# A macaron layer with routed experts: first FFN in groups of 1, 2, 3 and 2 sequences, a new order of loads and weight splits, ranks from products

## The chip, the core and the metric

The kernel runs on one core of a Trainium2 chip. The metric is the time of one execution on the device, in microseconds (us). A core has TensorE (PE, matrix products), VectorE (DVE), ScalarE (ACT), GpSimd (POOL) and SyncE (SP), each with its own instruction stream; they meet only at semaphores. DMA engines move data between the main memory and the on-chip memory.

## What is computed

```python
x = x + 0.5 * ffn(layernorm(x), gate_w, w1, w3, w2)
x = x + attn(layernorm(x), time_mix_k, time_mix_v, time_mix_r, time_decay, time_first, Wk, Wv, Wr, Wo)
x = x + 0.5 * ffn(layernorm(x), gate_w, w1, w3, w2)

def ffn(x, gate_w, w1, w3, w2):              # 8 experts, the best 2 of each token
    probs = softmax(x @ gate_w)
    expert_weights, expert_indices = top_k(probs, 2)
    expert_weights = expert_weights / expert_weights.sum(-1)
    for i in range(8):
        wi = where(expert_indices == i, expert_weights, 0).sum(-1)
        out += ((silu(x @ w1[i]) * (x @ w3[i])) @ w2[i]) * wi

def attn(x, ...):                            # linear attention with decay
    k, v, r = projections of x mixed with x shifted by one token
    # scan over the tokens: aa, bb, pp carry the weighted sums and their exponent
    return (sigmoid(r) * wkv(k, v)) @ Wo
```

x is 8 sequences of 512 tokens with 128 channels, the inner width of an expert 512, all float32. The layer norm has neither scale nor shift.

## The kernel before

Each token takes part in two experts, so its normalised row is copied twice into a list in main memory (`rows_in`) that is sorted by expert. The list is cut into tiles of 128 rows of one expert. A tile is loaded, turned (`turn_tile`, tensor pT), multiplied with w1 and w3 (`up`, tensors pa and pb), gated (`h`, L844) and multiplied with w2 (`down`, py); its rows go to `rows_out`, are gathered by token (L542) and added to x with their weights (`combine`, L854). The weights w1 and w3 are split into a high and a low float16 part first, ScalarE making the high one (`split_weights`, L570) and VectorE the low one (L827).

Sequences are handled in runs, each with its own list: `FIRST = (2, 2, 2, 2)` sequences in the first FFN, `SECOND = (3, 3, 2)` in the second. A run of 2 has 23 tiles, one of 3 has 31, one of 1 has 15: 177 tiles in seven runs. Before a run's first tile all of its rows must be in its list, and the list is filled with zeros first, since experts leave gaps. Runs share the four lists: run 4 uses that of run 0, run 5 that of run 1.

The routing of a run is the chain `pick`, `pick2` (best two experts on VectorE), `count` (TensorE: a product with a triangle of ones gives each token's rank within its block, one with all ones the totals), `place`, `place2` (VectorE: a running sum over blocks and experts, then each token's slot, L789), `scatter` (GpSimd, L528: for each block of 128 tokens and each of two choices one indirect DMA, 8 per sequence), `tiles` and `weights`. It needs `stats`, `rsqrt`, `norm`, `turn`, `logits`, `keep` of all its sequences. Between the two FFNs each sequence goes through the attention, the chain `MIX` from `combine` to `add` (L887 to L925 on VectorE), and the routing of runs 4 to 6 takes sequences only after it.

The order is made by `make_plan()` ahead of time, with costs in `COST` and allowances in `ROOM`: it walks over the tiles and puts steps behind them. What I call the list of a tile is the steps put behind it. Engines follow this order strictly: TensorE, ScalarE, VectorE and SyncE run `in_order`: tile, list, tile. The planner moves no tile on to within two of a run's start while that run's scatters are not given out, so a late routing makes one long list. GpSimd runs `TRANSFERS` in order; each has a gate, the number of products `h` that must be done. The steps marked `EARLY` come before the first tile. SyncE (L433) issues x, small inputs, zeros, staged weights, w2, the other zeros and x, then loads and stores of tiles; the load of a run's first tile waits for all of its scatters and is issued three loads ahead, so the stores behind it wait too. `rsqrt` (L693) is a chain of 13 small VectorE instructions, each waiting for the one before (`link`).

## Time and profile before

| | us |
|---|---|
| median of 3 runs | 689.54 (688.97 to 691.28) |
| the profiled execution | 690.3, its span 688.5 |
| TensorE busy | 518.2 (75% of the span) |
| VectorE busy | 430.6 (63%) |
| ScalarE busy | 334.9 (49%) |
| GpSimd busy | 264.7 (38%) |
| first product of a tile (`h`) starts | 75.74 |
| last one starts | 654.05 |

Times in the profile count from the span's start. A busy TensorE is a TensorE with matmuls under way. "Idle before" in brackets says how long an engine had been idle before an instruction, and what released it. An indirect DMA by GpSimd takes that engine about a microsecond of its own and lands later.

### The profile page before, as it was taken

The numbers are of one execution on the slowest core, as the hardware profiler recorded it, in microseconds if no ns is written. First come the engines' busy times: TensorE is split into PE (matmuls) and PEld (weight loads), VectorE is DVE, ScalarE is ACT, GpSimd is POOL, SyncE is SP. The second block draws the span as 40 slices with busy tenths as digits, with TensorE's granted clock in tenths as the row PEclk, the third lists the DMA queues.
The fourth block names the chain that finished last, engine by engine and source line by source line (L and its number), as shares of the span: only waits on it lengthen the run. The fifth ranks groups of instructions, "written<-read, shape, count | busy, mean of one in ns | idle before, by whom it ended". The sixth has DMA issues, their size and how long they took to land.

```text
span 688.5 us, 16328 instructions
## 1 busy us (share of the span) xinstructions
PE 518.2 (75%) x5128; PEld 462.3 (67%) x5128; DVE 430.6 (63%) x1314; ACT 334.9 (49%) x717; POOL 264.7 (38%) x267
## 2 busy tenths in 40 slices
PE   0300789899989889987962359989879989999920
PEld 0200679889878689765961139977769989999920
DVE  4490488675647599426987959786678683425402
ACT  0640546545584744777442435654856544444400
POOL 1067007556634320134101742415451547246244
PEclk9999999999999999999995579999998999999975
DMA  8991113223322222112100122221222333334222
GB/s 278 345 304 50 49 41 98 86 85 95 89 69 73 55 58 63 50 45 50 53 12 7 51 76 62 79 59 48 69 61 68 86 97 113 89 97 109 79 57 65
DMA packets 87564, 58.88 MB, mean 86 GB/s; under 512 B 9792, under 2 KB 81216, under 8 KB 87488
## 3 DMA queue, kind: packets, MB, share of 16 engines
q1 hardware_dynamic: 79296, 41.05, 20.3%
q0 software_dynamic: 8192, 16.79, 8.6%
q8 instruction: 50, 0.82, 0.5%
q14 instruction: 26, 0.21, 0.1%
HBM read 28.65 MB, written 29.16 MB: 84 GB/s over the span
## 4 chain that ended last, share of the span: by engine, by line
PE 26%; DVE 11%; POOL 6%; issue 5%; ACT 4%; DMA 2%; POOLq 0%; DVEq 0%; ACTq 0%
PE py L966 9%; PE pa L953 7%; PE pb L953 7%; POOL rows_in L528 4%; DVE h L844 2%; POOL yg L542 2%; DVE xres L854 1%; PE pT L941 1%; ACT L590 1%; ACT xn L608 1%; DMA rows_in<-parts,slot 1%; ACT sil L590 1%; DVE shared L915 1%; DMA rin<-rows_in 1%; DVE stats L687 0%
## 5 line engine op out<-in xcount | busy, mean ns | idle before, releaser
L844 DVE TENSOR_TENSOR h<-sil,pb 128x512 f32<-128x512 f32 x177 | 120.8, 687 | 177.7 <-ACT sil L590 130.7
L528 POOL DMA_INDIRECT rows_in<-parts,slot x128 | 136.9, 1070 | 210.4 <-DVE slot L789 81.7
L542 POOL DMA_INDIRECT yg<-rows_out,slot x128 | 125.9, 984 | 205.7 <-DVE h L844 158.4
L966 PE MATMUL py<-ffn_w,h 128*128 x1416 | 195.3, 282 | 7.6 <-ACT yrow L584 7.5
L966 PEld LDWEIGHTS py<-ffn_w,h 128*128 128x128 f32 x1416 | 175.1, 195 | 12.2 <-issue 8.2
L953 PE MATMUL pa<-rT,ffn_w 128*128 128x128 f16 (+1 forms) x1440 | 151.6, 248 | 21.1 <-ACT rT L579 10.9
L953 PE MATMUL pb<-rT,ffn_w 128*128 128x128 f16 (+1 forms) x1440 | 153.7, 247 | 0.0
L953 PEld LDWEIGHTS pa<-rT,ffn_w 128*128 x1440 | 114.5, 100 | 38.5 <-issue 26.9
L953 PEld LDWEIGHTS pb<-rT,ffn_w 128*128 x1440 | 114.7, 99 | 9.6
L590 ACT ACTIVATE sil<-pa 128x512 f32<-128x512 f32 x177 | 104.9, 593 | 22.5 <-PE pa L953 21.9
L584 ACT ACTIVATE yrow<-py 128x128 f32<-128x128 f32 x177 | 49.0, 277 | 114.3 <-PE py L966 113.1
L579 ACT ACTIVATE rT<-pT 128x512 f16<-128x512 f16 (+1 forms) x120 | 57.9, 482 | 85.1 <-PE pT L941 85.0
L941 PE MATMUL pT<-ident,rin 128*128 128x128 f16 x354 | 40.1, 222 | 49.9 <-DMA rin<-rows_in 49.9
L941 PEld LDWEIGHTS pT<-ident,rin 128*128 128x128 f16 x354 | 27.2, 99 | 52.1 <-DMA rin<-rows_in 50.4
L854 DVE SCALAR_TENSOR_TENSOR xres<-yg,wts,xres 128x128 f32<-128x128 f32 x128 | 36.4, 347 | 26.9 <-DMA yg<-rows_out,slot 26.3
L608 ACT ACTIVATE xn<-xres,shift,rstd 128x128 f32<-128x128 f32 x96 | 39.3, 482 | 10.1 <-DVE shift L703 10.1
L1005 PE MATMUL bkB<-xT,qkv_w 128*128 128x512 f16 x96 | 26.4, 415 | 3.1 <-ACT xT L636 2.4
L1020 PE MATMUL bkA<-ident,xn 128*128 128x128 f32 x64 | 11.6, 312 | 21.5 <-ACT xn L608 19.6
L1020 PEld LDWEIGHTS bkA<-ident,xn 128*128 128x128 f32 x64 | 8.9, 165 | 22.1 <-issue 19.5
L1041 PE MATMUL bkA<-ident,parts 128*128 128x128 f16 x64 | 6.1, 253 | 23.0 <-DVE rt L778 10.8
L687 DVE BATCH_NORM_STATS2 stats<-xres 128x6 f32<-128x128 f32 x96 | 20.8, 279 | 3.4 <-DMA xres<-in_x 3.2
L711 DVE TENSOR_TENSOR parts<-xn,parts 128x512 f16<-128x512 f32 x24 | 16.4, 689 | 9.9 <-ACT parts L620 9.5
(126 smaller groups left out, 454.1 us busy)
## 6 DMA issues: line engine op xcount, KB each, us to landing
rows_out<-yrow SPq DMA_DIRECT2D x177, 64.0 KB
rin<-rows_in SPq DMA_DIRECT2D x57, 128.0 KB
shared<-in_w SPq DMA_DIRECT2D x16, 256.0 KB, 6.0
rin<-rows_in SPq DMA_DIRECT2D x63, 64.0 KB
rows_in<-zrow SPq DMA_DIRECT2D x2, 1984.0 KB, 10.6
rows_in<-zrow SPq DMA_DIRECT2D x2, 1472.0 KB, 11.5
xres<-in_x SPq DMA_DIRECT2D x4, 512.0 KB, 7.4
ffn_w<-in_w SPq DMA_DIRECT2D x8, 256.0 KB, 6.5
```

Of the source, the lines that this page charges most:

```text
L528: pool.indirect_dma_start(rows_in[g][:], bass.IndirectOffsetOnAxis(ap=slot[:, c, at:at + 1], axis=0), parts[:, at, :], None).then_inc(s_sc ...
L542: pool.indirect_dma_start(yg[:, b, c, j, :], None, rows_out[SET[run]][0:STEPS[run] * T, :], bass.IndirectOffsetOnAxis(ap=slot[:, c, at:at ...
L579: act.activation(rT[:, q % 2, :, 0:n], pT[:, :, 0:n], ACT.Copy).then_inc(s_rT, 1)
L584: act.activation(yrow[:, t % YSLOTS, :], py[:], ACT.Copy).then_inc(s_yrow, 1)
L590: act.activation(sil[:, t % 2, :], pa[t % 2][:], ACT.Silu, scale=1.0 / WS).then_inc(s_sil, 1)
L608: ins = act.activation(xn[:, at, j, :], xres[:, js, :][:, j, :], ACT.Identity, bias=shift[:, u, j:j + 1], scale=rstd[:, u, j:j + 1])
L844: dve.tensor_tensor(h[:, t % RING, :], sil[:, t % 2, :], pb[t % 2][:], ALU.mult).then_inc(s_h, 1)
L854: ins = dve.scalar_tensor_tensor(xj, yg[:, b, c, j, :], wts[:, c, u * JU + j:u * JU + j + 1], xj, ALU.mult, ALU.add)
L941: mm = pe.transpose(pT[:, part, n * T:(n + 1) * T], rin[:, q % SLOTS, n, part * D:(part + 1) * D], ident16[:])
L953: mm = pe.matmul(bank[:, i * cols:(i + 1) * cols], weight_bytes[:, bass.ds(experts[q] * 4 + at, 2 * P)].bitcast(F16), rT[:, q % 2, xp, 0:c ...
L966: mm = pe.matmul(py[:], h[:, (FIRST_STEP[q] + c // per) % RING, at:at + T], w, start=(c == 0), stop=(c == FC - 1))
L1005: mm = pe.matmul(bank[:], qkv_w[:, f, wp, :], xT[:, u % 2, xp, start:start + S], start=(n == 0), stop=(n == 5))
```

## The change

- `FIRST` becomes (1, 2, 3, 2). Tiles start at 0, 15, 38 and 69 instead of 0, 23, 46 and 69; from 92 on the numbers are the same. List 2 grows from 23 to 31 tiles, as run 6 shares it in size only.
- Loads: x of run 0, gate, vectors, the weights of experts 0 and 1, x of run 1, the other six experts, then zeros. Of each list only what the first FFN needs is zeroed early; the rest (16 and 8 tiles of lists 0 and 1) comes after the other zeros. The three small inputs get a semaphore each, and att_w moves behind the first zeros.
- Weight splits become steps of the early order: expert 0 between `stats` and `rsqrt` of run 0, expert 1 behind `hi`, experts 2 and 3 between `logits` and `keep`, 4 to 7 behind run 0's routing. The statistics of run 1 come behind that routing. The split of the attention's weights moves behind the first copy on ScalarE and behind tile 1 on VectorE.
- Ranks: `count` sums blocks by products that accumulate, 2 x 4 per sequence instead of 2 in all, and `place` and `place2` lose the running sum over blocks (12 and 7 linked instructions instead of 22 and 9).
- `rsqrt` has 11 links instead of 13.

```diff
-FIRST = (2, 2, 2, 2)
+FIRST = (1, 2, 3, 2)
...
-COST = {"dve": {"combine": 2.8, "stats": 1.7, "mstats": 1.7, "rsqrt": 2.5, "mrsqrt": 2.5, "lo": 0.7, "lo_m": 0.7,
+COST = {"dve": {"combine": 2.8, "stats": 1.7, "mstats": 1.7, "rsqrt": 2.3, "mrsqrt": 2.3, "lo": 0.7, "lo_m": 0.7,
...
-                "att": 1.6, "add": 0.7, "pick": 1.6, "pick2": 1.8, "place": 4.0, "place2": 2.4, "tiles": 1.1,
+                "att": 1.6, "add": 0.7, "pick": 1.6, "pick2": 1.8, "place": 2.5, "place2": 1.6, "tiles": 1.1,
...
+    plan += [(EARLY, "split", 0, 0), (EARLY, "rsqrt", 0, 0)]
     plan += [(EARLY, step, 0, b) for b in early for step in ("norm", "hi")]
...
+    plan += [(EARLY, "split", 0, 1)]
+    plan += [(EARLY, "lo", 0, b) for b in early]
+    for b in early:
+        plan += [(EARLY, step, 0, b) for step in ("turn", "xnT", "logits")]
+        plan += [(EARLY, "split", 0, 2 + e) for e in range(2) if b == UNITS[0] - 1]
+        plan += [(EARLY, "keep", 0, b)]
+    plan += [(EARLY, step, 0, 0) for step, _ in CHOOSE]
+    plan += [(EARLY, "stats", 1, b) for b in one] + [(EARLY, "split", 0, 4), (EARLY, "rsqrt", 1, 0)]
+    plan += [(EARLY, "split", 0, e) for e in range(5, E)]
+    plan += [(EARLY, step, 1, b) for b in one for step in ("norm", "hi", "lo")]
...
+            def fill(g, start, end, filled):
+
+                rows = rows_in[g][start:end, :].rearrange("(r p) c -> p r c", p=P)
+                sp.dma_start(rows, zrow[:, None, :].to_broadcast([P, (end - start) // P, 2 * D])).then_inc(filled[g], 16)
...
             load_x(0)
+            sp.dma_start(gate_w[:], gate).then_inc(s_gate, 16)
+            sp.dma_start(vecs[:], channel_vecs).then_inc(s_vecs, 16)
+            stage(0)
+            stage(1)
+            load_x(1)
+            for e in range(2, E):
+                stage(e)
+            sp.wait_ge(s_zrow, 1)
+            fill(0, 0, STEPS[0] * T, s_fill)
+            sp.dma_start(att_raw[:], att_w).then_inc(s_attw, 16)
...
             for g in range(1, R1):
-                fill(g)
+                fill(g, 0, STEPS[g] * T, s_fill)
                 if g > 1:
                     load_x(g)
+            for g in range(SETS):
+                if ROWS[g] > STEPS[g] * T:
+                    fill(g, STEPS[g] * T, ROWS[g], s_rest)
...
-            act.wait_ge(s_small, 16 * 3)
+            act.wait_ge(s_vecs, 16)
...
+            def split(e):
+                act.wait_ge(s_stage[e], 32)
+                act.activation(up_w[:, e, 0::2, :], stage_w[:, :, e, :], ACT.Copy, scale=WS).then_inc(s_uphi, 1)
...
-                for _ in range(3):
-                    link(dve.tensor_tensor(w, r, r, ALU.mult))
-                    link(dve.scalar_tensor_tensor(w, w, -0.5, v, ALU.mult, ALU.mult))
-                    link(dve.scalar_tensor_tensor(r, w, 1.5, r, ALU.add, ALU.mult))
+
+                link(dve.tensor_tensor(w, r, r, ALU.mult))
+                link(dve.tensor_tensor(w, w, v, ALU.mult))
+                link(dve.scalar_tensor_tensor(w, w, -10.0 / 3.0, w, ALU.add, ALU.mult))
+                link(dve.scalar_tensor_tensor(r, w, 5.0, r, ALU.add, ALU.mult))
+
+                link(dve.tensor_tensor(w, r, r, ALU.mult))
+                link(dve.scalar_tensor_tensor(w, w, -0.5 / (third * third), v, ALU.mult, ALU.mult))
+                link(dve.scalar_tensor_tensor(r, w, 1.5, r, ALU.add, ALU.mult))
...
-                    cols = UNITS[run] * JU * E
-                    cv = chosen[:].rearrange("p j e -> p (j e)")[:, 0:cols]
-                    pe.matmul(bkB[:, 0:cols], ones16[:], cv, start=True, stop=True).then_inc(s_bfull, 1)
-                    pe.matmul(bkA[:, 0:cols], upper[:], cv, start=True, stop=True).then_inc(s_afull, 1)
+                    jg = UNITS[run] * JU
+                    flat = chosen[:].rearrange("p j e -> p (j e)")
+                    for j in range(jg):
+                        mm = pe.matmul(bkB[:, 0:E], ones16[:], flat[:, j * E:(j + 1) * E], start=(j == 0),
+                                       stop=(j == jg - 1))
+                    mm.then_inc(s_bfull, 1)
+
+                    pe.matmul(bkA[:, 0:jg * E], upper[:], flat[:, 0:jg * E], start=True, stop=False)
+                    for j in range(1, jg):
+                        mm = pe.matmul(bkA[:, j * E:jg * E], ones16[:], flat[:, 0:(jg - j) * E], start=False,
+                                       stop=(j == jg - 1))
+                    mm.then_inc(s_afull, 1)
```

SyncE's stream from its start, before (`xres` is x, `rows_in<-zrow` zeros, `shared<-in_w` staged weights, `ffn_w` w2, `rin` a tile's rows):

```order
L440 DMA xres<-in_x 128x8x128
L448 DMA gate_w<-in_gate 128x8
L449 DMA vecs<-in_channel_vecs 128x5
L440 DMA xres<-in_x 128x8x128
L444 DMA rows_in<-zrow 3968x1x256
L455 DMA shared<-in_w 128x512 x4
L457 DMA att_raw<-in_att_w 128x512
L455 DMA shared<-in_w 128x512 x12
L459 DMA ffn_w<-in_w 128x4x128 x8
```

and now, the last rows in full as far as the first tile's load:

```order
L459 DMA shared<-in_w 128x512 x12
L455 DMA rows_in<-zrow 128x15x256
L471 DMA att_raw<-in_att_w 128x512
L473 DMA ffn_w<-in_w 128x4x128 x8
L455 DMA rows_in<-zrow 128x23x256
L455 DMA rows_in<-zrow 128x31x256
L450 DMA xres<-in_x 128x12x128
L455 DMA rows_in<-zrow 128x23x256
L450 DMA xres<-in_x 128x8x128
L455 DMA rows_in<-zrow 128x16x256
L455 DMA rows_in<-zrow 128x8x256
L490 DMA rin<-rows_in 128x2x256 x3
```

The zeros of list 0 moved behind the staged weights, and two more fills stand ahead of the first tile's load.

VectorE around the slots of run 4 (96 columns: three sequences), before, in the list of tile 90, where no product `h` stands near:

```order
L769 TENSOR_TENSOR run_s<-run_s,cnt 128x96
L770 TENSOR_TENSOR run_s<-run_s,ne 128x96
L778 TENSOR_TENSOR rt<-bkA,run_s 128x96
L782 TENSOR_TENSOR rt<-rt,ne 128x96
L783 TENSOR_TENSOR rt<-rt,ne 128x96
L784 TENSOR_TENSOR rt<-rt 128x96
L786 TENSOR_TENSOR rt<-rt,pick 128x96 x2
L788 TENSOR_REDUCE slotf<-rt 128x12 x2
L789 CAST slot<-slotf 128x2x12
L794 TENSOR_TENSOR tcmp<-t_iota,ne 128x88
```

and now, behind tile 82, with products `h` (L864) ahead and behind:

```order
L864 TENSOR_TENSOR h<-sil,pb 128x512 x2
L796 TENSOR_TENSOR rt<-bkA,ne 128x96
L799 TENSOR_TENSOR rt<-rt,ne 128x96
L800 TENSOR_TENSOR rt<-rt,ne 128x96
L801 TENSOR_TENSOR rt<-rt 128x96
L802 TENSOR_TENSOR placed<-picks,rt 128x192
L804 TENSOR_REDUCE slotf<-placed 128x24
L805 CAST slot<-slotf 128x2x12
L709 BN_STATS stats<-xres 128x6 x4
L712 BN_AGGR mv<-stats 128x2 x4
L864 TENSOR_TENSOR h<-sil,pb 128x512
```

The routing of run 4 moved eight tiles ahead; in the plan 4 of its 24 scatters have gates up to tile 89 and 20 have that of tile 90.

VectorE around the slots of run 5, before, behind tile 109:

```order
L844 TENSOR_TENSOR h<-sil,pb 128x512 x2
L778 TENSOR_TENSOR rt<-bkA,run_s 128x96
L782 TENSOR_TENSOR rt<-rt,ne 128x96
L783 TENSOR_TENSOR rt<-rt,ne 128x96
L784 TENSOR_TENSOR rt<-rt 128x96
L786 TENSOR_TENSOR rt<-rt,pick 128x96 x2
L788 TENSOR_REDUCE slotf<-rt 128x12 x2
L789 CAST slot<-slotf 128x2x12
L844 TENSOR_TENSOR h<-sil,pb 128x512
```

and now, in the list of tile 121 (L924 to L934 are steps of the attention, `sum_a` to `divide`):

```order
L802 TENSOR_TENSOR placed<-picks,rt 128x192
L804 TENSOR_REDUCE slotf<-placed 128x24
L805 CAST slot<-slotf 128x2x12
L926 SCALAR_TENSOR_TENSOR shared<-shared 128x512
L927 TENSOR_TENSOR shared<-shared,vv 128x512
L810 TENSOR_TENSOR tcmp<-t_iota,pc 128x88
L812 TENSOR_TENSOR tcmp<-t_iota,sc 128x72
L815 TENSOR_REDUCE teid<-tcmp 128x20
L816 TENSOR_SCALAR eid<-teid 128x20
L826 TENSOR_SCALAR wts<-ed 128x12
L827 TENSOR_SCALAR wts<-ed 128x12
L929 TENSOR_TENSOR shared<-shared 128x512
```

The routing of run 5 moved from 14 tiles to 2 tiles ahead of its first tile, 123; all 24 scatters have the gate of tile 121 in the plan, where 5 had it before. In that list VectorE's two products `h` now stand 67 rows apart, with two thirds of two attention chains between them.

## Rows read from the trace of the kernel before

**Rows 1.** Windows: length, busy us of PE, PEld, DVE, ACT, POOL, clock, DMA, GB/s.

```profile
72.90:356.90 284.00, 259.23 (x2641) 232.24 (x2642) 194.56 (x588) 166.43 (x358) 96.48 (x96) 0.99 0.22 64
356.90:410.10 53.20, 17.43 (x82) 8.35 (x82) 42.42 (x153) 15.03 (x25) 23.88 (x24) 0.66 0.11 34
410.10:508.50 98.40, 91.03 (x867) 81.15 (x868) 74.28 (x207) 59.41 (x127) 38.05 (x38) 0.96 0.23 65
...
515.60:658.00 142.40, 139.03 (x1474) 131.54 (x1474) 74.89 (x188) 68.85 (x163) 62.07 (x64) 0.98 0.34 93
```

**Rows 2.** Timeline before tile 0: start, us, instruction, [idle before <- releaser].

```profile
17.69 0.20 ACT L564 ACTIVATE wdec<-vecs 128x1 f32<-128x1 f32 x1 [15.67 <-DMA att_raw<-in_att_w]
...
24.80 0.20 ACT L628 ACTIVATE logit<-bkB 128x32 f32<-128x32 f32 x1 [2.03 <-PE bkB L1026]
...
28.67 0.22 DVE L726 TENSOR_REDUCE mx<-logit 128x8 f32<-128x64 f32 x1 [3.10 <-ACT logit L628]
...
39.14 1.15 POOL L528 DMA_INDIRECT rows_in<-parts,slot  x1 [36.45 <-DVE slot L789]
...
41.29 4.40 SPq L440 DMA_DIRECT2D xres<-in_x  x1
...
42.79 9.16 DVE L827 SCALAR_TENSOR_TENSOR ffn_w<-shared,ffn_w 128x1024 f16<-128x1024 f32 x8
...
43.43 9.37 POOL L528 DMA_INDIRECT rows_in<-parts,slot  x1 [0.30 <-issue]
...
71.34 0.61 PE L941 MATMUL pT<-ident,rin 128*128 128x128 f16 x4 [39.13 <-DMA rin<-rows_in]
```

**Rows 3.** DMA issues, us to landing: scatters until 41.5, then the fourth.

```profile
rows_in<-parts,slot POOLq DMA_INDIRECT x2, 5.8
...
rows_in<-parts,slot POOLq DMA_INDIRECT x1, 10.6
```

**Rows 4.** Windows of the traffic at the start, columns as in rows 1.

```profile
28.00:50.00 22.00, 0.61 (x4) 0.38 (x4) 19.52 (x68) 12.93 (x21) 9.95 (x4) 1.00 1.12 331
50.00:52.00 2.00, 0.00 (x0) 0.00 (x0) 1.96 (x2) 0.00 (x0) 2.00 (x1) 1.00 0.01 3
```

**Rows 5.** Timeline of VectorE: products h of tiles 0, 5 and 14.

```profile
75.74 0.69 DVE L844 TENSOR_TENSOR h<-sil,pb 128x512 f32<-128x512 f32 x1 [22.65 <-PE pb L953]
...
92.22 0.69 DVE L844 TENSOR_TENSOR h<-sil,pb 128x512 f32<-128x512 f32 x1
...
115.39 0.68 DVE L844 TENSOR_TENSOR h<-sil,pb 128x512 f32<-128x512 f32 x1
```

**Rows 6.** Timeline behind tile 89 and in the list of tile 90.

```profile
352.58 0.69 DVE L844 TENSOR_TENSOR h<-sil,pb 128x512 f32<-128x512 f32 x1 [1.83 <-ACT sil L590]
...
367.63 0.26 DVE L746 COPY cnt<-bkB 128x96 f32<-128x96 f32 x1
...
375.67 1.00 POOL L528 DMA_INDIRECT rows_in<-parts,slot  x1 [45.28 <-DVE slot L789]
...
381.69 0.49 DVE L894 TENSOR_SCALAR shared<-shared,wdec 128x512 f32<-128x512 f32 x1
...
402.55 0.48 DVE L896 TENSOR_SCALAR shared<-shared,wdec 128x512 f32<-128x512 f32 x1
...
405.62 0.96 POOL L528 DMA_INDIRECT rows_in<-parts,slot  x1 [0.30 <-issue]
...
410.08 0.61 PE L941 MATMUL pT<-ident,rin 128*128 128x128 f16 x4 [7.13 <-DMA rin<-rows_in]
```

**Rows 7.** Timeline behind tile 121.

```profile
508.45 0.69 DVE L844 TENSOR_TENSOR h<-sil,pb 128x512 f32<-128x512 f32 x1 [0.40 <-ACT sil L590]
...
515.56 0.61 PE L941 MATMUL pT<-ident,rin 128*128 128x128 f16 x4 [3.63 <-DMA rin<-rows_in]
```

**Rows 8.** A timeline row of twelve products, and a group of all instructions of L701.

```profile
507.29 0.83 PE L953 MATMUL pb<-rT,ffn_w 128*128 128x128 f16 x12
...
L701 DVE SCALAR_TENSOR_TENSOR nwt<-nwt,var 128x4 f32<-128x4 f32 (+1 forms) x66 | 10.8, 163 | 2.3
```

More of the change, by code:

```diff
@@ L201, in make_plan @@
                                                   if c.steps is CHOOSE and c.run < run)
-                        or any(step in COST[eng] and load[eng] >= ROOM[eng] for eng in COST)):
+                        or run != 1 and any(step in COST[eng] and load[eng] >= ROOM[eng] for eng in COST)):
                     break
@@ L614, in step @@
                 me = (name, run, b)
+                if name == "split":
+                    split(b)
                 if name in NORMS:
```

147 lines of the change are left out of this document (67 added, 80 removed).

## The prediction

> **What bounds the kernel now.** I read the profile in this order: the busy time of the engines by stretches, then the timeline where TensorE is idle, then who released it. Between the first tile and the last, from 72.9 to 658 us, TensorE is busy except in two places [rows 1]. In the tile stretches it is busy 259.2 of 284.0 us, 91.0 of 98.4 and 139.0 of 142.4: 35.6 us idle in 525, so a tile costs what its matmuls cost. The exceptions are the 53.2 us behind tile 90, with 17.4 us of TensorE, and 6.4 us behind tile 121 [rows 7]. There, and before the first tile, TensorE waits for scattered rows. So the time is a start (71.3 us), TensorE's own work, two waits for scatters, and a tail of 30 us that the change doesn't touch. The change leaves the number of tiles at 177 and of runs at seven. What it does to the time is how it moves these waits.
>
> **The start.** Before, ScalarE waits for att_w until 17.69, the slots of two sequences release the first of 16 scatters at 39.14, and tile 0's rows are turned at 71.34 [rows 2]. The fourth scatter lasts 9.37 us, beside the eight weight splits that VectorE runs back to back from 42.79 to 51.95; it ends 0.85 us after them, which is about a scatter's usual 0.96 us. A split takes 9.16 / 8 = 1.15 us; the change puts four of them (experts 4 to 7) behind the slots, so I let them hold the scatters for 5 us. The Trainium skill has a rule for this (SBUF — State Buffer, "SBUF: two separate sides"): descriptors of a GpSimd DMA are written through a port that some VectorE instructions lock for as long as they run. The trace agrees in this one place; without the rule the hold could be a full DMA queue instead, and last as long as the queue is full.
>
> After: x of one sequence is 0.25 MB instead of 0.5 MB, and the split of expert 0 stands between statistics and square root, so I put the first shift at 12 us (estimate: stage 0 lands near 7.5, then a ScalarE and a VectorE split of 1.0 and 1.2, then 11 links of 0.2). From there to the logits kept it was 7.2 us for a sequence (17.8 to 25.0), plus two splits now: 21. From the first reduction to the first scatter it was 10.5 us (28.67 to 39.14) [rows 2]; shorter ranks and 32 instead of 64 elements take 2.8 of it: first scatter at 28.5. Eight scatters at the 1.5 us of the first three, and 5 us of being held by splits, end near 45.5 to 46; landing took 5.8 us for the first two and 10.6 for the held one [rows 3], so they are in by 52.
>
> But SyncE has to issue everything that stands ahead of the first row load, and the same rings have to carry it. Before, its last issue ended at 45.69 [rows 2] and traffic stopped at 50: 331 GB/s from 28 to 50, 3 GB/s in the next 2 us [rows 4]. The change adds 8 tiles of zeros (116 instead of 108, 64 KB each, 0.52 MB) and four more scatters inside this stretch (0.26 MB): at 340 GB/s 2.3 us, so 52.3. Tile 0's load stands behind that, and lands at 53.3. The Trainium skill says the same of the order (DMA: Bandwidth & Descriptors, "Queues, rings and completion order"): descriptors on a ring are taken in order. No row of before shows a load behind zeros, and without that order the rows could be in 1 us earlier. Routing (52) and queue (53.3) thus end together; I take the queue. ScalarE now also makes qkv's high part behind the first copy, 0.3 us. Start: 71.34 - 53.3 - 0.3 = **17.7 us less** (bounds: 20, if the queue drains at 50; 8, in the rival below).
>
> **Tile 14.** The first run has 15 tiles now, and sixteen scatters of run 1 have to land before tile 15 is turned. Product of tile 5 came 16.5 us after that of tile 0 [rows 5]; place and place2 take 4.3, a scatter follows 0.4 later, 21.9 us behind tile 0; 15 more at 1.27 give 40.9, and from the last scatter's start to the turned rows it was 4.46 us (405.62 to 410.08) [rows 6]: 45.4. Without a wait that turn would stand at 38.4 (the product of tile 14 at 39.65, less 1.3), plus 2.2 for the norm work that now comes there. That is 4.8 idle, and about 0.7 for a lower clock after it: **+5.5** (0 to 9). Run 2 ends its scatters one tile before they are due: **+1** (0 to 2.3).
>
> **Behind tile 90.** Before, routing of run 4 stands in this list, because its third sequence was mixed late. From the product of tile 89 (353.27) to the turn of tile 92 (410.08) it is 56.8 us [rows 6], of which 15.7 at full clock is work. Now run 4 is routed at tile 82 and only 20 of its scatters stand behind product 89: 19 intervals of 1.302 (29.95 over 23) and 4.46: 29.2, say 29.4. The list's VectorE work, which hides under it, is about the 21.3 us from one sequence's gaps to the next one's (381.69 to 403.03) [rows 6]. Work inside is 13.0. Idle falls from 41.1 to 16.4: **-24.7** (-20 to -27).
>
> **Behind tile 121.** Before, 6.4 us from the product's end at 509.14 to the turn at 515.56 [rows 7], 3.2 of it idle. Run 5 needs sequence 5. It was the second of run 2 and is now the third, so its mix comes last of three; the routing slips from tile 109 to the list of tile 121, and all 24 scatters with it. Sum: sum_a 2.0, place and place2 4.5 (before, from 367.63 to just before 375.67, 7.2; twelve instructions fewer) [rows 6], 0.8 until the scatter starts as before it, then 29.95 and 4.46: 41.7. VectorE's list is 36.5 us by the same rows and fits beneath. Work inside is 6.3, so 35.4 idle instead of 3.2: **+32.2** (+28 to +36).
>
> **Products for ranks.** 128 small matmuls take the place of 14. Their price is not in the trace; the nearest is the stream of 12 weight loads and products of 128 columns in 0.83 us, 69 ns each [rows 8]; from below it is bounded by nothing at all, if TensorE's idle 7% swallows it, from above by a weight load of 100 ns. 28 of the 114 more lie in waits. 86 at 69 ns is 5.9; two thirds of it exposed: **+4** (0 to 8.6). The Trainium skill gives 81 ns for such a stream (TensorE: Matmul & The Clock Gate, "Back-to-back issue gap"); by that it would be 4.6, the row decides.
>
> **VectorE.** A square root loses two of 13 links (22 of them before, as L701 runs three times in each) [rows 8], place ten, place2 two: some 26 us of VectorE's 431, off the path except where TensorE waits for it in the tile stretches. I take **-4** of the 35.6 idle (+3 to -12; the lists behind tiles 72 and 73, where two mixes ran together, are also thinner now, those behind 53 to 60 thicker). Edits of buffers and of the semaphores for small loads cost nothing else.
>
> **Sum.** -17.7 - 24.7 + 32.2 + 5.5 + 1 + 4 - 4 = -3.7 on a span of 688.5: 684.8. The profiled run took 690.3, the median of the runs is 689.54; the difference goes on the median: **685.8 us**.
>
> **Rivals.** (a) Slower: the first scatters are held. Place: the eight scatters of run 0. If one of them is held for 9.4 us, as the fourth was, and the later ones land after 10.6, the last starts at 50 and tile 0 is turned at 62.7: the start gives 8.3, the total is 695.2. For it speaks that splits and a full DMA queue lie beside all eight now; against it, that no more than four splits are left and never more than three in a row. It decides the case once the last scatter starts later than about 46; every microsecond behind that costs one. (b) No change: VectorE's saving is worth nothing to TensorE, as its idle time is made by lists that are just regrouped: 689.8. For it: VectorE is off the path in the tile stretches. (c) Clearly faster: TensorE's idle share in tiles 0 to 90 nearly halves (24.8 us) [rows 1], as the mixes no longer run in pairs behind tile 72: 676. Against it: they run in pairs behind tile 53. (d) The change doesn't do what it says: grouping decides less than the planner's due times; that is in the forecast, as the wait that leaves tile 90 comes back at 121.
>
> **Chances.** Forecast 0.43 (681 to 687.4), (a) 0.23, (b) 0.22, (c) 0.12. A measurement of this kernel can tell some 0.3%, 2.1 us, from no change: faster by more is the forecast and (c), 0.55; within it (b), 0.22; slower (a), 0.23. The range reaches from (c) to (a), 677 to 696. The likeliest case's own is 681 to 688.
>
> **What would show it.** Tile 0 turned at 52 to 55, with traffic at 340 GB/s until 52; slots at 26 to 30. A wait of 3 to 7 us at tile 14. The product of tile 89 to the turn of tile 92 in 28 to 31 us. From the product of tile 121 to the turn of tile 123 40 to 43, with 24 scatters in it and VectorE done before them. It would be wrong if tile 0 starts later than 57, if VectorE's list rather than the scatters ends the wait at 121, or if the tile stretches lose or win more than 6 us of TensorE's idle time.

## The result, and the profile after

The changed kernel takes **683.2 us** (median; 680.6 to 686.3) where the kernel before, timed beside it, takes 690.4 (688.9 to 692.3): a ratio of 0.990, with a 95% interval of 0.987 to 0.993. The forecast was 685.8 with a range of 677 to 696, and faster. The profiled execution took 680.58, with a span of 678.4 (688.5 before). It is the fastest of the seven, 2.6 us under their median, while that of before took 690.3, close to its own; so the two spans differ by 10.1 us and the two medians by 7.2. In the medians of the experiments, executions over 1.5% slower than the fastest of their kernel are left out.

Windows of the changed kernel, with the columns of rows 1: tile 0's first products to the wait for rows behind tile 14; to the product of tile 89; to the turn of tile 92; to the product of tile 121; to the turn of tile 123; to the tail.

```profile
54.40:102.00 47.60, 41.53 (x471) 38.93 (x472) 34.32 (x152) 30.25 (x74) 15.79 (x16) 0.96 0.18 52
102.00:333.20 231.20, 215.12 (x2211) 195.93 (x2212) 153.86 (x441) 128.53 (x283) 90.26 (x92) 0.97 0.25 71
333.20:363.60 30.40, 15.19 (x91) 9.19 (x89) 24.07 (x52) 11.48 (x20) 20.85 (x20) 0.73 0.16 51
363.60:463.70 100.10, 92.29 (x890) 82.48 (x890) 72.79 (x195) 69.87 (x138) 16.57 (x16) 0.96 0.18 51
463.70:505.30 41.60, 10.62 (x63) 6.14 (x63) 32.13 (x73) 7.37 (x13) 24.13 (x24) 0.58 0.14 43
505.30:648.00 142.70, 139.24 (x1488) 132.15 (x1488) 61.98 (x162) 67.07 (x158) 61.09 (x64) 0.98 0.33 93
```

Where [rows 1] had one long hole behind tile 90, there are two now, of 30.4 and 41.6 us. The last stretch is what it was.

The start, answering [rows 2]: VectorE's slots and its last three splits, the first and the three last of eight scatters, and tile 0's turn.

```profile
25.23 0.17 DVE L805 CAST slot<-slotf 128x8 int32<-128x8 f32 x1
...
25.70 1.15 POOL L546 DMA_INDIRECT rows_in<-parts,slot  x1 [23.01 <-DVE slot L805]
...
32.09 3.49 DVE L831 SCALAR_TENSOR_TENSOR ffn_w<-shared,ffn_w 128x1024 f16<-128x1024 f32 x3
...
32.43 1.71 POOL L546 DMA_INDIRECT rows_in<-parts,slot  x1 [0.31 <-issue]
34.44 1.96 POOL L546 DMA_INDIRECT rows_in<-parts,slot  x1 [0.30 <-issue]
36.71 0.96 POOL L546 DMA_INDIRECT rows_in<-parts,slot  x1 [0.30 <-issue]
...
53.02 0.61 PE L968 MATMUL pT<-ident,rin 128*128 128x128 f16 x4 [31.47 <-DMA rin<-rows_in]
```

The traffic, answering [rows 4]. It no longer stops at 50 but past 52:

```profile
28.00:50.00 22.00, 0.00 (x0) 0.00 (x0) 10.35 (x36) 4.44 (x10) 7.84 (x7) 1.00 1.14 351
50.00:52.00 2.00, 0.00 (x0) 0.00 (x0) 0.00 (x0) 0.00 (x0) 0.00 (x0) 1.00 1.15 346
52.00:54.00 2.00, 0.61 (x4) 0.34 (x4) 0.00 (x0) 0.33 (x1) 0.00 (x0) 1.00 0.38 113
```

The turns that wait for scattered rows, behind tile 14, before the third group's first tile (38), before tile 92 and before tile 123, and ahead of the last two the last of their scatters (answering [rows 6, 7]). The bracket holds the idle time of TensorE right before.

```profile
101.93 0.61 PE L968 MATMUL pT<-ident,rin 128*128 128x128 f16 x4 [5.10 <-DMA rin<-rows_in]
...
172.45 0.61 PE L968 MATMUL pT<-ident,rin 128*128 128x128 f16 x4 [2.81 <-DMA rin<-rows_in]
...
359.14 0.96 POOL L546 DMA_INDIRECT rows_in<-parts,slot  x1 [0.30 <-issue]
363.60 0.61 PE L968 MATMUL pT<-ident,rin 128*128 128x128 f16 x4 [4.18 <-DMA rin<-rows_in]
...
462.99 0.69 DVE L864 TENSOR_TENSOR h<-sil,pb 128x512 f32<-128x512 f32 x1 [4.03 <-ACT sil L608]
...
470.79 1.17 POOL L546 DMA_INDIRECT rows_in<-parts,slot  x1 [60.95 <-DVE slot L805]
...
500.98 0.96 POOL L546 DMA_INDIRECT rows_in<-parts,slot  x1 [0.30 <-issue]
505.29 0.61 PE L968 MATMUL pT<-ident,rin 128*128 128x128 f16 x4 [20.57 <-DMA rin<-rows_in]
```

Cut at these points, the two spans differ so:

| stretch | before | after | measured | by the forecast |
|---|---|---|---|---|
| start to tile 0's turn | 71.3 | 53.0 | -18.3 | -17.7 |
| to the end of product 89 | 281.9 | 280.2 | -1.8 | +6.1 with the two other tile stretches |
| to the turn of tile 92 | 56.8 | 30.4 | -26.4 | -27.4 |
| to the end of product 121 | 99.1 | 100.1 | +1.0 | (above) |
| to the turn of tile 123 | 6.4 | 41.6 | +35.2 | +35.3 |
| to the end | 172.9 | 173.1 | +0.2 | (above) |
| sum | 688.5 | 678.4 | -10.1 | -3.7 |

(The forecast counted idle time for the two waits, -24.7 and +32.2; as lengths of the stretches its figures are 56.8 to 29.4 and 6.4 to 41.7, so 0.4 of work leaves the tile stretches: 5.5 + 1 + 4 - 4 - 0.4 = 6.1.) Nearly all that the forecast missed lies in the tile stretches: -0.6 instead of +6.1. The start (0.6 more) and the wait behind tile 90 (1.0 less) nearly cancel.

### The profile page after: what moved, and what is told of

Read it like the earlier page. It is cut to its first block, busy times and chain, and to the rows that moved or that the text cites. A ratio compares the mean times of both kernels' runs of the same rounds, so it can differ in the third digit from the quotient of the medians.

```text
span 678.4 us, 16446 instructions
## 1 busy us (share of the span) xinstructions
PE 519.3 (77%) x5242; PEld 469.0 (69%) x5242; DVE 411.4 (61%) x1206; ACT 332.6 (49%) x715; POOL 255.5 (38%) x267
## 4 chain that ended last, share of the span: by engine, by line
PE 58%; POOL 9%; DVE 8%; issue 7%; SPq 7%; ACT 6%; DMA 4%; POOLq 0%; ACTq 0%; DVEq 0%
PE py L993 20%; PE pb L980 15%; PE pa L980 15%; POOL rows_in L546 7%; PE pT L968 3%; DMA rin<-rows_in 2%; POOL yg L560 2%; PE bkB L1032 2%; SPq L455 2%; SPq L450 2%; DVE h L864 2%; ACT xn L626 1%; DMA rows_in<-parts,slot 1%; PE bkB L1053 1%; ACT L608 1%
## 5 line engine op out<-in xcount | busy, mean ns | idle before, releaser
L864 DVE TENSOR_TENSOR h<-sil,pb 128x512 f32<-128x512 f32 x177 | 121.2, 687 | 192.4 <-ACT sil L608 135.5
L546 POOL DMA_INDIRECT rows_in<-parts,slot x128 | 130.4, 1018 | 214.1 <-DVE slot L805 84.0
L560 POOL DMA_INDIRECT yg<-rows_out,slot x128 | 123.3, 963 | 201.2 <-DVE h L864 154.2
L980 PEld LDWEIGHTS pa<-rT,ffn_w 128*128 x1440 | 116.1, 100 | 28.1 <-issue 16.7
L874 DVE SCALAR_TENSOR_TENSOR xres<-yg,wts,xres 128x128 f32<-128x128 f32 x128 | 36.4, 347 | 26.9 <-DMA yg<-rows_out,slot 26.3
L1090 PE MATMUL bkA<-att_raw,shared 128*128 128x128 f32 x64 | 11.3, 334 | 16.3 <-DVE shared L940 16.3
L1090 PEld LDWEIGHTS bkA<-att_raw,shared 128*128 128x128 f32 x64 | 10.3, 244 | 17.2 <-issue 17.2
```

The source lines that it names most:

```text
L546: pool.indirect_dma_start(rows_in[g][:], bass.IndirectOffsetOnAxis(ap=slot[:, c, at:at + 1], axis=0), parts[:, at, :], None).then_inc(s_sc ...
L560: pool.indirect_dma_start(yg[:, b, c, j, :], None, rows_out[SET[run]][0:STEPS[run] * T, :], bass.IndirectOffsetOnAxis(ap=slot[:, c, at:at ...
L864: dve.tensor_tensor(h[:, t % RING, :], sil[:, t % 2, :], pb[t % 2][:], ALU.mult).then_inc(s_h, 1)
L874: ins = dve.scalar_tensor_tensor(xj, yg[:, b, c, j, :], wts[:, c, u * JU + j:u * JU + j + 1], xj, ALU.mult, ALU.add)
L980: mm = pe.matmul(bank[:, i * cols:(i + 1) * cols], weight_bytes[:, bass.ds(experts[q] * 4 + at, 2 * P)].bitcast(F16), rT[:, q % 2, xp, 0:c ...
```

## The experiments

They ran in four sets, each with the kernel before timed beside it: runs 1 to 4 on chip 7, runs 5 to 8 and runs 9 to 11 on chip 9, run 12 on chip 11. The chip of the result isn't on record; by the times I take it for another. In all four sets the kernel before is slower than beside the result, at 751.7, 758.3, 752.4 and 750.4 us, and so is the changed kernel where it ran again, in run 5. What is known of it comes at the end. So a run is read against the kernel before, or a neighbour, of its own set, and its time not against 683. "Ratio" is a run's time over that of the kernel before of its set, with a 95% interval. How far a ratio can be trusted from set to set is shown by two kernels with the same plan for all tiles, the second and the twelfth run: 0.989 and 0.999, though the twelfth starts 1.7 us earlier. Below 1% I compare within a set only.

### 1. The groups of before in the changed kernel

```diff
-FIRST = (1, 2, 3, 2)
+FIRST = (2, 2, 2, 2)
```

> The changed kernel with FIRST = (2, 2, 2, 2) again; loads, splits, ranks and square root stay changed. My theory (the time is start plus waits for scatters): tile 0 is turned near 58 instead of 53, as 16 scatters at 1.27 us follow slots at 32; the wait at tile 14 (5.1 us) goes, the wait behind tile 90 grows back from 30 to 57 us, the wait behind tile 121 falls from 41.6 to 6 us: 683 + 5 - 5.5 + 26.4 - 35.2 = 674 us. Rival (the smaller first group carries the gain): undoing it costs the 18 us of the start, 690 us or more.

Measured: 749.8, ratio 0.998 (0.994 to 1.001). Tile 0's rows are turned at 59.51, 6.5 later than with a group of one. The wait behind tile 14 is gone, behind tile 121 the gap between products is 16 us, and the long wait behind tile 90 is back: product to product 53 us, the turn at 428.39. So the groups are what moves the waits. But the time doesn't fall by the 9 us that my theory gave: against the kernel before it is the same. The absolute times expected were worked out from the 683 of the result, and can't be read here or in runs 2 to 4.

### 2. The new groups alone

The kernel before with `FIRST = (1, 2, 3, 2)` and nothing else.

> The kernel before with FIRST = (1, 2, 3, 2) alone. My theory: slots near 34.5, since ScalarE waits for att_w and ranks are long; eight scatters of which one is held by the eight splits in a row for some 9 us, tile 0 turned near 58 instead of 53; the wait behind tile 121 is 2.7 us longer (place); small matmuls save 4, VectorE costs 4: 691 us. Rival (the full DMA queue sets the start anyway, loads and splits in their new order bring nothing): tile 0 turned at 53 to 54, 686 us.

Measured: 744.2, ratio 0.989 (0.984 to 0.994), from four executions. Tile 0 is turned at 54.98 (58 expected), 16.4 us earlier than before, and the whole change turns it only 2.0 earlier still. That doesn't make the rest of the change worth 2 us: run 1 has all of it but the groups, and its 59.51 is 11.8 us earlier than before. Each by itself brings most of the 18.3 us. The larger waits stand where the changed kernel has them, with 7.71 us idle behind tile 14. The one behind tile 121 is shorter, 38.4 us from product to turn and not 41.6 (I had expected 2.7 more): with the costs of before in the planner the slots are ready 2.5 us behind product 121, in the changed kernel 6.3.

In this set the groups alone bring as much as the whole change brings beside its own kernel before (0.991 in the fifth run), and the change without them, run 1, has 0.998. But the same groups with the same plan have 0.999 in run 12, and in run 6 taking them away costs 1.5 us, within the intervals. So what the groups are worth in time, between nothing and the whole gain, stays open.

### 3. The zeros of the second pass behind the first row loads

```diff
-            for g in range(SETS):
-                if ROWS[g] > STEPS[g] * T:
-                    fill(g, STEPS[g] * T, ROWS[g], s_rest)
...
             for q in range(SLOTS):
                 load(q)
+            for g in range(SETS):
+                if ROWS[g] > STEPS[g] * T:
+                    fill(g, STEPS[g] * T, ROWS[g], s_rest)
```

> The changed kernel with the zeros that only the second FFN needs (24 tiles, 1.57 MB) issued behind the first three tile loads. If the DMA queue sets the start (my theory), tile 0 is turned 4.6 us earlier, near 48.5, and the time falls by as much, to 678.7. If routing and scatters set it, tile 0 stays at 53 and the time at 683.

Measured: 744.8, ratio 0.992 (0.989 to 0.995). The turn of tile 0:

```profile
48.79 0.50 PE L968 MATMUL pT<-ident,rin 128*128 128x128 f16 x3 [27.54 <-DMA rin<-rows_in]
```

4.2 us earlier than 53.02, at 48.79 where 48.5 was expected, with the scatters where they were (the eighth at 36.4). So it was the queue that held tile 0's load in the changed kernel, and not the scatters: 24 tiles of zeros less ahead of it bring the turn forward by 4.2 us, where 1.57 MB at the 340 GB/s of the forecast are 4.6. The wait behind tile 121 is the same 41.6 us. Whether the time falls by 4.2 us can't be said, as the changed kernel itself isn't in this set.

### 4 and 7. The ranks of before in the changed kernel

The old `place`, `place2` and two wide products for each routing are back, under the changed planner's costs. The core of the edit:

```diff
-                    for j in range(jg):
-                        mm = pe.matmul(bkB[:, 0:E], ones16[:], flat[:, j * E:(j + 1) * E], start=(j == 0),
-                                       stop=(j == jg - 1))
-                    mm.then_inc(s_bfull, 1)
...
+                    pe.matmul(bkB[:, 0:cols], ones16[:], cv, start=True, stop=True).then_inc(s_bfull, 1)
+                    pe.matmul(bkA[:, 0:cols], upper[:], cv, start=True, stop=True).then_inc(s_afull, 1)
```

> The changed kernel with count, place and place2 as before the change (14 small matmuls instead of 128, 12 more linked VectorE instructions per routing), order of steps unchanged. My theory: the start stays (hidden under the queue), the wait behind tile 121 is 2.7 us longer, the tile stretches lose 4 us of matmuls and gain 3 of VectorE: 685. Rival A (the small matmuls cost nothing): 688 to 689. Rival B (VectorE's saving brings nothing in the tile stretches): 682.

> The changed kernel with the counts, scans and ranks of before (two products of 64 or 96 columns instead of up to 24, longer place and place2 on VectorE), now beside the changed kernel. The prediction had the products at +4 and VectorE at -4 together for ranks and square root. By the measured products (0.48 us for 12 into one bank) the ranks part is a gain: this kernel is 3 to 8 us slower than the changed one, of which 2.7 behind tile 121. Rival (as sized on record): within 2 us of the changed one. The first four runs (762.6 beside 744 to 750 for its neighbours) point to 12 us or more, which would need a cause outside the routing steps.

Measured: 762.6 in the first set (ratio 1.016 [1.010, 1.022]; its neighbours 744 to 750), and 764.0 in the second (1.007 [1.002, 1.012]), where the changed kernel itself took 752.6: 11 us slower, more than the 3 to 8 that I expected. Both sets agree, so it is no chance. The turns of tiles 92 and 123 in run 4, and then in run 3 of the same set, whose tiles are the changed kernel's (tile 0 is turned at 52.84 and 48.79):

```profile
406.19 0.60 PE L982 MATMUL pT<-ident,rin 128*128 128x128 f16 x4 [5.33 <-DMA rin<-rows_in]
...
553.06 0.61 PE L982 MATMUL pT<-ident,rin 128*128 128x128 f16 x4 [20.54 <-DMA rin<-rows_in]
```

```profile
396.41 0.61 PE L968 MATMUL pT<-ident,rin 128*128 128x128 f16 x4 [5.27 <-DMA rin<-rows_in]
...
539.39 0.61 PE L968 MATMUL pT<-ident,rin 128*128 128x128 f16 x4 [20.55 <-DMA rin<-rows_in]
```

From turn 0 to turn 92 it takes 353.4 instead of 347.6, from there to turn 123 146.9 instead of 143.0, and to the end 202.6 instead of 200.5: +5.7, +3.9, +2.1. It is spread over all stretches that hold a routing, not only behind tile 121.

### 5. The changed kernel itself

> The changed kernel itself, beside the three that follow it on the same chip, so that they are read against it and not against the kernel before. Theory (the gain is the earlier start, the two waits cancel, the tile stretches give a little): ratio to before 0.985 to 0.995; tile 0 turned at 53.0, waits for rows behind tile 14 (5.1 us), behind tile 89 (30.4 from h to the next turn) and behind tile 121 (41.6). Rival (on the chip of the first four runs before took 751 us with the same code, so the gain may depend on the chip): the ratio is 1.00 or more on such a chip.

Measured: 752.6, ratio 0.991 (0.987 to 0.995). The gain in per cent is that of the result. Tile 0 is turned at 53.14, and the waits stand where they did: 4.98, 2.85, 5.41 and 20.74 us idle before the turns at 110.31, 191.59, 398.90 and 541.62.

### 6. The groups of before, now beside the changed kernel

> The changed kernel with the four groups of 2 sequences of before, now beside the changed kernel. By the regrouping theory: tile 0 turned at 59.5 (6.5 later than 53.0), no wait behind tile 14 (-5.1), the wait behind tile 90 back to some 50 (+20) and the one behind tile 121 nearly gone (-35 to -41): 13 to 26 us below the changed kernel. Rival, by the first four runs (749.8 beside 744.2 for the groups alone): the groups themselves are worth what the change gains, and this one is 5 us slower than the changed kernel; then the tile stretches must cost more in it, and the stage that does is seen in the gaps between the h.

Measured: 754.1, ratio 0.994 (0.990 to 0.998); the changed kernel's 0.991 lies inside. My 13 to 26 us don't come. By the profiles the start costs 5.6 more (turn at 58.78), tile 0 to tile 92 21.4 more (367.1 beside 345.8), from there to product 122 26.1 less (119.8 beside 145.9) and the rest 5.6 less: -4.7 on the span, +1.5 in the median. The step that fell is the wait behind tile 121. Without it that stretch is 26 us shorter, not 35 to 41, since a gap of 14.5 us stays there (531.2 to 545.7). The start costs what I had counted; tile 0 to tile 92 costs 21.4 where the waits that I had counted make 15. The profile is of this kernel's fastest execution, 5.5 us under its median, so the stretches are read for where the waits stand and not for the sum.

### 8. A denser plan, meant to remove both waits

```diff
-FIRST = (1, 2, 3, 2)
+FIRST = (2, 2, 2, 2)
...
-ROOM = {"dve": 2.1, "act": 1.8}
-RATE = 1.6
+ROOM = {"dve": 2.8, "act": 2.2}
+RATE = 2.0
```

with the zeros of run 3's edit.

> A plan meant to remove both late waits: the changed kernel in groups of 2, 2, 2, 2, the planner's room per step raised from 2.1 to 2.8 (VectorE) and 1.8 to 2.2 (ScalarE), its transfer rate from 1.6 to 2.0, and the zeros of the second pass queued behind the first tile loads. Theory: the waits behind tiles 90 and 121 are below 10 us together (from 68 us that stand there in the changed kernel between h and turn), tile 0 is turned at 55 to 56: 30 to 45 us below the changed kernel. Rival: steps crowded into fewer tiles push h late on VectorE, each tile costs 0.1 to 0.2 us more and the gain is 5 to 20; or the chain of steps itself, and not the room, sets when the last scatters go, and both waits stay.

Measured: 756.5, ratio 0.995 (0.991 to 1.000), nothing of the 30 to 45 us: it is 4 us slower than the changed kernel. The waits are gone: no turn but tile 0's (58.82, expected 55 to 56) waits for rows, and no gap between two products is over 11.4 us, where the changed kernel has 30.3 and 45.7. Yet from the first product to the last it takes 653.9 us beside 659.5. The windows of this kernel and of the changed kernel, first product to last:

```profile
65.10:718.97 653.87, 537.75 (x5156) 472.76 (x5155) 373.14 (x1053) 296.47 (x666) 221.09 (x224) 0.93 0.22 61
```

```profile
57.39:716.86 659.47, 532.07 (x5176) 472.64 (x5175) 379.53 (x1073) 307.81 (x679) 230.25 (x232) 0.92 0.21 61
```

TensorE is idle 116 us of the one and 127 of the other, so most of the idle time was moved, not removed. Where it sits shows in ScalarE's waits (engine, line, releaser: us in all, times, longest), dense plan first:

```profile
ACT yrow L602 <- remote: 78.5, 24, 6.4
...
ACT rT L597 <- remote: 44.2, 15, 4.7
```

```profile
ACT yrow L602 <- remote: 45.3, 17, 6.5
ACT rT L597 <- remote: 33.8, 15, 3.5
```

"remote" stands for a release that nothing recorded on this core explains. Over all of ScalarE's lines it is 147 us in the dense plan and 87 in the changed kernel. In the two traces of the result there isn't one such row. What the dense plan gives where there are none was not measured.

### 9. The old ranks with their own costs in the planner

```diff
-                "att": 1.6, "add": 0.7, "pick": 1.6, "pick2": 1.8, "place": 2.5, "place2": 1.6, "tiles": 1.1,
+                "att": 1.6, "add": 0.7, "pick": 1.6, "pick2": 1.8, "place": 4.0, "place2": 2.4, "tiles": 1.1,
```

on top of run 4's edit.

> The changed kernel with the ranks of before and, this time, the planner's costs of before for them too (place 4.0 and place2 2.4 instead of 2.5 and 1.6), so that the plan leaves them the room that they need. Theory (the 13 us that the old ranks cost under the new costs, 765.6 beside 752.6, come from a plan that gives VectorE 2.3 us too little at each of the seven routings, so h waits for it): here they cost 0 to 4 us over the changed kernel's ratio of 0.9906, that is 0.990 to 0.996, less or more by how the waits at the starts of groups move with the plan. Rival (the ranks themselves are 13 us dearer wherever they stand): ratio 1.00 to 1.01.

Measured: 743.9, ratio 0.990 (0.983 to 0.997), from four executions. The old ranks had 1.007 in run 7 and the changed kernel 0.991 in run 5, both on the same chip but in the other set; so the 11 us are gone, by two numbers of the planner. The waits moved too: none is left behind tile 14, and the last two are shorter, 0.93 and 6.64 us idle before the turns at 395.86 and 536.81, where the changed kernel had 5.41 and 20.74. So no run shows that ranks from products are worth anything once the plan knows what its steps cost. That the 11 us came from a plan that gives each routing 2.3 us too little is my reading. The two numbers also moved the waits, and how much came back by either isn't told apart. The new ranks under the old costs were not run.

### 10. All eight splits in a row behind the first routing

```diff
-    plan += [(EARLY, "split", 0, 0), (EARLY, "rsqrt", 0, 0)]
+    plan += [(EARLY, "rsqrt", 0, 0)]
...
-    plan += [(EARLY, "split", 0, 1)]
...
-        plan += [(EARLY, "split", 0, 2 + e) for e in range(2) if b == UNITS[0] - 1]
...
-    plan += [(EARLY, "stats", 1, b) for b in one] + [(EARLY, "split", 0, 4), (EARLY, "rsqrt", 1, 0)]
-    plan += [(EARLY, "split", 0, e) for e in range(5, E)]
+    plan += [(EARLY, "stats", 1, b) for b in one] + [(EARLY, "rsqrt", 1, 0)]
+    plan += [(EARLY, "split", 0, e) for e in range(E)]
```

> The changed kernel with all eight weight splits behind the first routing, one after the other on VectorE, as before the change; the order of the loads stays. It tests the rival in which one of the first scatters is held. Theory: the scatter that is under way when the splits begin is held until the last of them ends, 9.4 us instead of 1.7 and 2.0, the eighth is issued at 43 to 45 instead of 36.7, and tile 0 is still turned at 53.0, since the zeros in the queue set it: ratio within 0.003 of the changed kernel's 0.9906. Rival: tile 0 is turned 3 us or more later and the ratio is 0.995 or more; or no scatter is held over 3 us, and the long hold of before had another cause.

Measured: 747.4, ratio 0.994 (0.991 to 0.998), a little outside the 0.003, tile 0 turned at 53.36. Of the theory the second half holds: the turn stays. The first half falls: the eighth scatter starts at 34.87, not at 43 to 45. The eight splits on VectorE and the scatters beside them:

```profile
25.70 9.16 DVE L829 SCALAR_TENSOR_TENSOR ffn_w<-shared,ffn_w 128x1024 f16<-128x1024 f32 x8
...
26.45 1.30 POOL L544 DMA_INDIRECT rows_in<-parts,slot  x1 [0.30 <-issue]
28.06 1.97 POOL L544 DMA_INDIRECT rows_in<-parts,slot  x1 [0.31 <-issue]
30.33 1.97 POOL L544 DMA_INDIRECT rows_in<-parts,slot  x1 [0.30 <-issue]
32.60 1.96 POOL L544 DMA_INDIRECT rows_in<-parts,slot  x1 [0.30 <-issue]
```

None is held over 1.97 us. Against the 1.26 from one scatter's start to the next elsewhere (359.14 back to 357.88 in the changed kernel), the starts here are 2.27 apart, about two splits of 1.15.

### 11. The denser plan with the new groups

`ROOM` 2.4 and 2.2, `RATE` 2.0, `FIRST = (1, 2, 3, 2)`, and the zeros of run 3's edit.

> The changed kernel with the planner's room at 2.4 (VectorE) and 2.2 (ScalarE), the transfer rate at 2.0 and the zeros of the second pass behind the first tile loads. On the chip of the last eight runs the denser plan for groups of 2 took all the late waits away (68 us) and gained only what ScalarE and VectorE lost again in short idle stretches with no releaser on this core (155 us on ScalarE beside 90). Theory: on a chip where before takes about 752 to 758 us it is the same here, ratio 0.985 to 1.00; on one where before takes 690 us, with no such stretches, the gain of the removed waits stays, ratio 0.94 to 0.97. Tile 0 turned at 48.8; waits behind tiles 91 and 122 together under 20 us. Rival: crowded steps cost the tiles as much on either chip, ratio 0.985 or more on both.

Measured: 751.0, ratio 0.997 (0.993 to 1.002). Tile 0 is turned at 48.79, one wait of 6.81 us is left before the turn at 405.88, and ScalarE's "remote" waits add up to 130 us. It is the theory's first branch. The second, that the gain stays on a chip without such waits, and the rival, that crowding costs as much everywhere, are still not told apart, as the traces of all these sets have such waits.

### 12. The mixing weights behind the splits

In the kernel before with the new groups alone, VectorE's ten small operations on the mixing weights (`omix`, `wdec`, `wfull`, `qkv_f`) are moved from ahead of the eight splits to behind them:

```diff
+                for e in range(E):
+                    dve.wait_ge(s_uphi, e + 1)
+                    dve.scalar_tensor_tensor(up_w[:, e, 1::2, :], stage_w[:, :, e, :], WS, up_w[:, e, 0::2, :],
+                                             ALU.mult, ALU.subtract).then_inc(s_uplo, 1)
                 dve.tensor_scalar(omix[:], vecs[:, 0:3], -1.0, 1.0, ALU.mult, ALU.add)
...
-                for e in range(E):
-                    dve.wait_ge(s_uphi, e + 1)
-                    dve.scalar_tensor_tensor(up_w[:, e, 1::2, :], stage_w[:, :, e, :], WS, up_w[:, e, 0::2, :],
-                                             ALU.mult, ALU.subtract).then_inc(s_uplo, 1)
```

> The kernel before with groups of 1, 2, 3 and 2 alone, as in the second run, but with VectorE's ten small operations on the mixing weights behind its eight weight splits instead of ahead of them. In the kernel before and in the second run the fourth scatter was held 9.37 us, to 0.85 us behind the last of eight splits; with eight splits in a row in the changed kernel no scatter was held over 1.97. Theory (something that the small operations right ahead of the splits take stays with VectorE as long as it runs without a gap): without them ahead no scatter is held over 2.0 us, the eighth scatter starts at 41 to 43 instead of 49.8. Rival (the hold is the eight splits' own): 9.4 us again, from a scatter begun in the first split. In both tile 0 is turned at 54 to 55.5 and the ratio is 0.985 to 0.995, as in the second run.

Run 2, with the small operations ahead:

```profile
35.54 0.28 DVE L822 TENSOR_SCALAR qkv_f<-att_raw,omix 128x128 f32<-128x128 f32 x1
35.74 9.16 DVE L827 SCALAR_TENSOR_TENSOR ffn_w<-shared,ffn_w 128x1024 f16<-128x1024 f32 x8
...
36.37 9.37 POOL L528 DMA_INDIRECT rows_in<-parts,slot  x1 [0.30 <-issue]
```

Run 12, with them behind:

```profile
33.52 9.17 DVE L818 SCALAR_TENSOR_TENSOR ffn_w<-shared,ffn_w 128x1024 f16<-128x1024 f32 x8
...
34.76 1.96 POOL L528 DMA_INDIRECT rows_in<-parts,slot  x1 [0.30 <-issue]
37.02 1.97 POOL L528 DMA_INDIRECT rows_in<-parts,slot  x1 [0.30 <-issue]
39.29 1.97 POOL L528 DMA_INDIRECT rows_in<-parts,slot  x1 [0.30 <-issue]
41.56 1.97 POOL L528 DMA_INDIRECT rows_in<-parts,slot  x1 [0.30 <-issue]
```

The same eight splits for the same 9.16 us: 9.37 us of hold for one scatter with the small operations ahead, 1.97 for each of four without. The eighth scatter starts at 45.1 instead of 49.8 (41 to 43 expected: four are slowed, where I had counted on fewer), and tile 0 is turned at 53.24 instead of 54.98. The ratio is 0.999 (0.995 to 1.002), outside what I expected; the profiles put it between first and last product, 655.6 us beside 648.3 with the same plan. That is why I trust no ratio to better than 1% from one set to another.

## Why the prediction was right, point by point

**The start** was right in size, and the queue was rightly chosen. Slots at 25.4 (26 to 30 forecast), tile 0 turned at 53.02 (53.3), first product 18.5 us earlier (75.74 to 57.27). That the queue and not the routing sets it was a choice between two ends that the forecast had 1.3 us apart; run 3 shows it, as less ahead of the load brings the turn forward to 48.79. The end of the routing was badly off, without harm: in the changed kernel the last scatter started at 36.71 and not at 45.5. I had let four splits hold them for 5 us, and had taken 1.5 us a scatter where most take 1.26. Neither term reached the sum. The Trainium skill's statement that descriptors on a ring are taken in order (DMA: Bandwidth & Descriptors, "Queues, rings and completion order") agrees with run 3.

**Rival (a)**, a scatter held for 9.4 us, didn't happen: 1.71 and 1.96 beside three splits. Run 10 shows that eight splits in a row at this place don't bring it either. Even run 2, with the long hold, has tile 0 turned at 54.98, since its rows are turned not 10.6 us behind the last scatter's start, but 5.2.

**Tile 14** waited 5.10 us (4.8 forecast), turned 44.7 us behind the first product (45.4). **The third group** (run 2 of the lists, from tile 38) waited 2.81 (1 forecast, up to 2.3): its scatters were not a tile early but late. **Behind tile 90**: 30.4 us from product to turn (29.4); I had taken 1.302 between scatters and from these 20 it was 1.35, from 333.47 to 359.14. **Behind tile 121**: 41.6 (41.7), with 24 scatters from 470.79 to 500.98 and VectorE's list done before them, as said.

**Mis-sized was the pair of terms for products, +4, and VectorE, -4, together nothing.** Measured, the tile stretches beyond the two small waits come to -0.6 - 7.9 = -8.5, of which -0.4 is the work that left: -8.1 instead of 0. Of this up to 2.6 us can be the luck of the profiled execution, the fastest of seven; in which stretch, no trace tells. The windows from tile 0's turn to product 89, before and after:

```profile
71.34:353.27 281.93, 256.99 (x2618) 230.05 (x2619) 191.03 (x578) 165.58 (x355) 96.48 (x96) 0.99 0.23 65
```

```profile
53.02:333.19 280.17, 257.24 (x2685) 235.21 (x2686) 188.18 (x593) 159.50 (x358) 106.05 (x108) 0.97 0.24 67
```

TensorE is busy for as long, 257.0 and 257.2 us, though it issues 67 matmuls more. It was idle 24.9 us and is idle 22.9, of which 7.9 are the two waits: 15.0 without them, 9.9 less. That is what **rival (c)** said, that TensorE's idle share in these tiles nearly halves, and nearly its size (some 10); I had given it 0.12. It is also a sign of being wrong that the prediction named itself: by [rows 1] and the windows above, the idle time of the tile stretches fell from 35.5 us to 33.4, of which 7.9 are the new waits, so without them TensorE won 10 us, more than the 6 allowed. That the time still came within 3 us of the forecast is in part luck: the new waits were 1.4 us longer than forecast, the one behind tile 90 1.0, and the stretches behind tile 92 gave nothing back. With the 114 extra products TensorE's busy time in the whole span is only 1.1 us higher (518.2 to 519.3). A stream of small ones is cheap:

```profile
464.10 0.48 PE L1062 MATMUL bkB<-chosen,ones 128*128 128x8 bf16 x12 [4.43 <-ACT xT L656]
```

40 ns each, where I had taken 69 from products of 128 columns [rows 8]: an error of the row chosen, columns do matter. VectorE's busy time falls from 430.6 to 411.4, 19 us instead of 26.

What made the 9.9 us can't be laid to one edit. The regrouped lists, the shorter steps and the plan that the shorter costs allow came together. Runs 4, 7 and 9 show that the old steps under the new costs lose 11 to 18 us and, in the next set on the same chip, nothing measurable under their own. Run 2 leaves open whether the groups alone give the whole gain, by the 0.999 of run 12. So **rival (b)**, that VectorE's saving is worth nothing to TensorE, isn't refuted as a mechanism; as a forecast of no change in time it failed. **Rival (d)** was in the forecast and came true: -26.4 behind tile 90, +35.2 behind tile 121.

## What to carry to other kernels

When a planner works from costs written by hand, a step's true length and its cost have to change together: the same steps were 11 us slower with costs 2.3 us too low for each routing. Splitting the first group smaller shortens the start, but savings at one place don't add up: here the groups alone took 16.4 us off it, the rest of the change alone 11.8, both together 18.3. It also shifts which chain is last at each later hand-over, so each must be worked out to its last scatter. The large gains and losses here (18, 26, 35 us) could all be read from the trace of before to about 1 us, and the sum was off by what no single wait shows. For a first load, count what stands ahead of it in its queue before shortening the work that it waits for.

## What the chip showed that I had not expected

**The long hold of a scatter.** The Trainium skill says (SBUF — State Buffer, "SBUF: two separate sides") that a port shared by VectorE and GpSimd is locked for a whole instruction. The 1.97 us of runs 10 and 12 fit that, a scatter of 0.96 that waits for the split under way; the 9.37 us of run 2 and of the kernel before don't, since they outlast seven ends of splits. (The prediction took them as agreeing with the page.) One scatter waits for the whole row only where `qkv_f`'s small operations stand directly ahead of it. It isn't just any small operation: in run 10 the links of a square root stand there, and no scatter takes over 1.97 us. ScalarE's cast of `qkv_f` moves with them in run 12, so which of the two it is stays open, and so does the mechanism.

**The same program takes 9 to 10% longer in the four sets than in the result, in single stretches.** Tiles 56 to 71 of the changed kernel, where GpSimd issues nothing, in the result and in run 5:

```profile
235.83:285.04 49.21, 46.12 (x486) 41.83 (x487) 37.29 (x65) 24.82 (x53) 0.00 (x0) 0.97 0.16 46
```

```profile
261.60:310.92 49.32, 47.45 (x486) 42.03 (x487) 37.28 (x65) 24.90 (x53) 0.00 (x0) 0.97 0.16 46
```

And product 122 to the last, with 48 gathers and 16 scatters:

```profile
508.47:644.02 135.55, 133.08 (x1444) 126.32 (x1444) 61.29 (x162) 64.03 (x153) 61.09 (x64) 0.99 0.33 91
```

```profile
544.80:716.86 172.06, 146.67 (x1445) 135.00 (x1445) 61.88 (x161) 62.58 (x153) 61.42 (x64) 0.93 0.26 72
```

49.2 and 49.3 us, but 135.6 and 172.1. VectorE, ScalarE and GpSimd are busy for as long in both. TensorE is busy 13.6 us longer, at a granted clock of 0.93 instead of 0.99, and idle 22.9 us longer. What is added on the other engines are waits of up to 6.5 us like this one, in run 5. TensorE's four turns for a tile are over at 136.83, and ScalarE, which waits for them, and SyncE, which waits too, start together at 139.3:

```profile
136.44 0.39 PE L968 MATMUL pT<-ident,rin 128*128 128x128 f16 x4
...
139.31 0.32 SPq L490 DMA_DIRECT2D rin<-rows_in  x1
139.32 0.60 ACT L597 ACTIVATE rT<-pT 128x512 f16<-128x512 f16 x1 [3.37 <-remote]
```

In run 5 every such row lies beside transfers issued by GpSimd. So it looks as if signals between engines arrive late there while GpSimd issues. I haven't shown that, and not that it belongs to the chip: the result was also measured at another time. It may be why a plan with more work per tile gained nothing in runs 8 and 11; that crowding costs as much everywhere is the other explanation, and no run decides between them.
